# Six of sixteen states with both drive halves turned by TensorE, the other ten by GpSimd, in a Mamba scan

## The chip, the cores and the metric

The kernel runs on one core of one Trainium2 chip. The metric is the device time of one execution in microseconds. The engines are PE (TensorE, with weight loads shown as PEld), DVE (VectorE), ACT (ScalarE), POOL (GpSimd) and SP (SyncE, which here only issues DMAs). They run side by side and meet through semaphores.

## The reference

The input is x, 8 sequences of 256 tokens with 128 channels. Layer 0 is a Mamba block in both directions and a mixture of experts, layer 1 is an attention block and a second mixture. The change lies in the Mamba scan:

```python
dt = softplus(dtr @ Wdt + bdt)                  # 256 inner channels
A = -exp(Alog)                                  # 256 channels x 16 states
h = exp(dt_t * A) * h + (dt_t * u_t) * B_t      # for each of 16 states
y_t = sum over states of h * C_t
```

The first factor is called the decay here, and the product dt * u * B the drive. B and C have one value for each token and state, and dt * u one for each token and channel.

## The kernel before

**Tiling.** Tokens lie along the free axis, 512 of them (two sequences) at a time, and 128 channels on the partitions, so the 256 inner channels are two halves. Four pairs of sequences in two directions give eight groups. Each has 16 states, so `N` runs from 0 to 127 and `q = 2 N + half` counts 256 scans. State `j` is `N % 16`.

**One state.** ACT computes the decay of each half by an Exp with a scale per partition (`state`, L761). DVE scans each half over 512 tokens (`scan`, L1074): half 0 into PSUM (`ps`), half 1 into SBUF (`moe`). DVE multiplies half 0 by C (`times_c`, L1082, result `hc`) and POOL does so for half 1 (L575). PE adds both, transposed, into y (`add_y`, L1621), three states later (`LAG`). POOL counts its products in `hc_pooled`, and the scan of half 1 of state N waits until the product of state N - 2 is done, since `moe` has two buffers.

**The drives.** GpSimd makes a drive by multiplying `dtu` (dt * u) by a row of B that a DMA spread over all partitions (`drive_half`, L567). In three states of four (`turned`) half 0 comes another way: `dtuT` holds dt * u with tokens on the partitions, where B is a column, so ACT scales four blocks of 128 x 128 by a column of `bT` (`scale_drive`, L777, result `scaled`), and PE transposes them into the PSUM bank that the scan will overwrite (`turn_drive`, L1601). So a group has 12 turned halves and 20 by GpSimd.

**Order.** One list of events sets the order on every engine. PE has the events of a slot ahead of the state with that number, the other engines behind it. A slot holds the work for the next group: u at slots 0 to 3 (`part` and `u`), y of the group before at 4 and 5, z at 6 and 7 (with two table loads on ACT, L710 and L716), `finish` at 8, x at 9, dt of half 0 and 1 at 11 and 13 (DVE adds at L1057, then POOL makes `dtu`, L644), b at 14 (PE L1555, ACT L719) and t at 15 (PE L1559, ACT L721 copies into `dtuT`). In the last groups parts of the next layer's norm (`n`) and a transpose of xn (`xt`) stand in slots 10 to 14. All these share one PSUM bank, `side`. DVE multiplies the finished y by the gate (`gate_y`, L1110) inside state 3, between the two scans. A wait holds all that is behind it on its engine.

**GpSimd's order.** At state N it makes the drives of state N + 2, with the product of half 1 of state N - 1 between them.

Of the kernel before, what the change touches and what calls it, by code (L numbers as in the profile page):

```python
# [19 lines left out]
ALU = mybir.AluOpType  # L20
# [80 lines left out]
def timeline():  # L101
# [180 lines left out]
DECAYS, SB_DECAYS = 3, 2  # L282


def decay_before(q):

    n = (POOLED.index(q) - DECAYS) if pooled_drive(q) else (TURNED_Q.index(q) - SB_DECAYS)
    return -1 if n < 0 else (POOLED if pooled_drive(q) else TURNED_Q)[n]

# [5 lines left out]
def build(nc, a, out):  # L295
    with ExitStack() as ctx:
# [45 lines left out]
        dtuT = sb("dtuT", [P, COLS])  # L342
# [26 lines left out]
        drive = sb("drive", [P, DRIVES + 2, COLS])  # L369
        decay_sb = sb("decay_sb", [P, SB_DECAYS, COLS])  # L370
        scaled = sb("scaled", [P, 2, COLS])
# [71 lines left out]
        def drive_of(N, half):  # L443
            return drive[:, N % DRIVES] if half else drive[:, DRIVES + N // 4 % 2]
# [16 lines left out]
        def _(sp):  # L461
# [30 lines left out]
            def load_b(N):  # L492
                after(sp, "drive_ready", drives_before(HALVES * max(N - B_RING + 1, 0)))
                sp.dma_start(b_sb[:, N % B_RING], bc_rows[N // STATES, N % STATES].partition_broadcast(P)) \
                    .then_inc(sem[f"b_loaded{N % B_RING}"], 16)
# [20 lines left out]
            for N in range(ALL):  # L516
                if N % STATES == 0:
                    store_bc(N // STATES)
                load_b(N)
# [16 lines left out]
        def _(pool):  # L536
# [27 lines left out]
            def drive_half(N, half):  # L564
                pool.wait_ge(sem[f"b_loaded{N % B_RING}"], 16 * (N // B_RING + 1))
                after(pool, "scan_done", 2 * (N - (DRIVES if half else 8)) + half + 1)
                pool.tensor_tensor(drive_of(N, half), dtu[:, N // STATES % 2, half], b_sb[:, N % B_RING], ALU.mult) \  # L567
                    .then_inc(sem["drive_ready"], 1)
# [30 lines left out]
            for ev in MAIN_READERS:  # L599
# [18 lines left out]
                elif ev[0] == "state":  # L618
                    N = ev[1]
                    if N == 0:  # L620
                        pool.wait_ge(sem["dtu_ready"], HALVES)
                        for first in range(DRIVES - 1):
                            for half in range(HALVES):
                                if half or first and not turned(first):
                                    drive_half(first, half)
                    M = N + DRIVES - 1
                    if M < ALL:
                        if M % STATES == 0:
                            pool.wait_ge(sem["dtu_ready"], HALVES * (M // STATES + 1))
# [4 lines left out]
                    if M < ALL:  # L634
                        drive_half(M, 1)
                elif ev[0] == "dt":
# [5 lines left out]
                    if g > 1:  # L642
                        pool.wait_ge(sem["side_ready"], SIDE["t", g - 2] + 1)
# [25 lines left out]
        def _(act):  # L669
# [29 lines left out]
            def side_part(ev):  # L699
# [20 lines left out]
                elif kind == "t":  # L720
                    act.activation(dtuT[:], side, ACT.Copy).then_inc(sem["side_free"], 1)  # L721
# [45 lines left out]
            def scale_drive(N):  # L767
# [4 lines left out]
                act.wait_ge(sem["side_free"], SIDE["t", g] + 1)  # L772
# [227 lines left out]
        def _(dve):  # L1000
# [58 lines left out]
            def scan(N, half):  # L1059
                q = 2 * N + half  # L1060
                dve.wait_ge(sem["decay_ready"], q + 1)
                if half:
                    dve.wait_ge(sem["drive_ready"], drives_before(q + 1))
                    after(dve, "hc_pooled", shared_before(q) - 1)
                    source = drive_of(N, 1)
                elif turned(N):
                    dve.wait_ge(sem["drive_turned"], turned_before(N) + 1)
                    source = h_of(q)
                else:
                    dve.wait_ge(sem["drive_ready"], drives_before(q + 1))  # L1070
                    after(dve, "hc_ready", N - OWN_H + 1)
                    source = drive_of(N, 0)
# [16 lines left out]
            def state(N):  # L1089
# [7 lines left out]
                scan(N, 1)  # L1097
# [4 lines left out]
                times_c(N)  # L1102
# [366 lines left out]
        def _(pe):  # L1469
# [58 lines left out]
            def project(ev):  # L1528
# [27 lines left out]
                elif kind == "t":  # L1556
                    pe.wait_ge(sem["dtu_ready"], HALVES * g + 1)
                    for t in range(4):
                        last = pe.transpose(side[:, t * P:(t + 1) * P], dtu[:, g % 2, 0, t * P:(t + 1) * P], ident[:])  # L1559
# [32 lines left out]
            def turn_drive(N):  # L1592
# [3 lines left out]
                after(pe, "hc_ready", N - OWN_H + 1)  # L1596
                if N == 1:
                    pe.wait_ge(sem["side_free"], SIDE["dt", 0, 1] + 1)
                for t in range(4):
                    block = slice(t * P, (t + 1) * P)  # L1600
                    last = pe.transpose(ps[:, H_BANKS[N % OWN_H], block], scaled[:, n % 2, block], ident[:])  # L1601
# [420 lines left out]
```

## Time and profile before

| what | value |
|---|---|
| time, median of 3 runs | 864.05 us (862.56 to 867.24) |
| the profiled execution | 863.14 us |
| its span, from first to last instruction | 860.6 us |
| mean granted TensorE clock | 0.897 |
| PE busy | 688.3 us, 80% |
| DVE busy | 584.9 us, 68% |
| ACT busy | 601.6 us, 70% |
| POOL busy | 417.7 us, 49% |

The scan stage lies between about 120 and 578 us of the span. Busy time is the union of an engine's instructions. Starts and durations in rows of the view in order of time are microseconds from the start of the span; a bracket at a row's end tells how long its engine was idle and what ended the wait.

### The profile page before, as it was taken

To read this page: it belongs to the slowest core of one execution; us is meant where nothing else is said; L and a number is where in the kernel's file an instruction comes from. 1 tells how busy PE (TensorE), PEld (TensorE's weight loads), DVE (VectorE), ACT (ScalarE), POOL (GpSimd) and SP (SyncE) were. 2 spreads that over 40 slices of the span, in tenths; PEclk is the share of its full clock that TensorE was granted. 3 is DMA by queue.
4 is the path that set the end of the run, shared out by engine and by line. 5 is a ranking of instruction groups with operands and counts; after the bars stand their busy time and mean duration, and the time that the engine had idled before them with its cause. 6 is when DMAs were issued, how large, how long until landed. Compare 5 with 4: busy or idle time off the path is not lost.

```text
span 860.6 us, 13106 instructions
## 1 busy us (share of the span) xinstructions
PE 688.3 (80%) x4227; PEld 482.5 (56%) x4227; DVE 584.9 (68%) x851; ACT 601.6 (70%) x1235; POOL 417.7 (49%) x359
## 2 busy tenths in 40 slices
PE   5799956797886877977768675768797888888886
PEld 5588835575674565655636645767683333334433
DVE  6335669897997987979878868796325455545542
ACT  3444559878888888789887987774645667765663
POOL 4300058797896987978968778770000000000000
PEclk8889979799797997999987967889999999999998
DMA  3224525454453553644634436710200000000000
GB/s 108 99 66 132 179 100 169 135 166 144 135 186 111 156 170 119 182 137 147 189 100 142 164 109 175 249 60 1 74 26 1 1 1 1 1 1 1 13 14 24
DMA packets 48130, 85.78 MB, mean 100 GB/s; under 512 B 6320, under 2 KB 11448, under 8 KB 48064
## 3 DMA queue, kind: packets, MB, share of 16 engines
q1 hardware_dynamic: 48064, 84.96, 31.6%
q8 instruction: 34, 0.56, 0.3%
q14 instruction: 32, 0.26, 0.1%
HBM read 83.37 MB, written 1.57 MB: 99 GB/s over the span
## 4 chain that ended last, share of the span: by engine, by line
PE 34%; ACT 26%; issue 14%; DVE 10%; POOL 1%; DVEq 0%; POOLq 0%; ACTq 0%
ACT scaled L777 6%; ACT ps L761 5%; PE ps L1621 4%; ACT decay_sb L761 3%; PE ps L1570 3%; PE ps L1911 3%; PE ps L1880 2%; PE ps L1601 2%; PE ps L1888 2%; DVE ps L1074 2%; PE ps L1919 2%; PE ps L1615 2%; PE ps L1821 1%; DVE moe L1074 1%; DVE hc L1082 1%
## 5 line engine op out<-in xcount | busy, mean ns | idle before, releaser
L567 POOL TENSOR_TENSOR drive<-dtu,b_sb 128x512 f32<-128x512 f32 x160 | 203.3, 1278 | 0.7
L575 POOL TENSOR_TENSOR hc<-moe,c_sb 128x512 f32<-128x512 f32 x128 | 166.0, 1297 | 42.8 <-DVE moe L1074 42.2
L1074 DVE TENSOR_TENSOR_SCAN moe<-ps,drive 128x512 f32<-128x512 f32 x128 | 153.3, 1198 | 0.2
L1621 PEld LDWEIGHTS ps<-ident,hc 128*128 128x128 f32 x1024 | 133.2, 157 | 32.4 <-issue 27.4
L1621 PE MATMUL ps<-ident,hc 128*128 128x128 f32 x1024 | 150.7, 299 | 0.0
L1074 DVE TENSOR_TENSOR_SCAN ps<-decay_sb,ps 128x512 f32<-128x512 f32 x96 | 117.5, 1224 | 39.5 <-PE ps L1601 22.7
L981 ACT ACTIVATE probs<-ps 128x1024 f32<-128x1024 f32 (+1 forms) x96 | 87.8, 916 | 74.3 <-PE ps L1888 64.2
L1601 PE MATMUL ps<-ident,scaled 128*128 128x128 f32 x384 | 68.7, 308 | 71.3 <-ACT scaled L777 69.0
L777 ACT ACTIVATE scaled<-dtuT,bT 128x128 f32<-128x128 f32 x384 | 121.4, 389 | 0.0
L761 ACT ACTIVATE ps<-dt,negA 128x510 f32<-128x510 f32 x160 | 105.9, 676 | 1.8 <-DVE ps L1086 1.2
L580 POOL TENSOR_TENSOR stat<-stat,halfc 128x4 f32<-128x4 f32 x7 | 7.0, 1007 | 201.0 <-DVE stat L1297 201.0
L1601 PEld LDWEIGHTS ps<-ident,scaled 128*128 128x128 f32 x384 | 49.5, 157 | 85.4 <-ACT scaled L777 84.2
L1082 DVE TENSOR_TENSOR hc<-ps,c_sb 128x512 f32<-128x512 f32 x128 | 85.0, 664 | 0.0
L761 ACT ACTIVATE decay_sb<-dt,negA 128x510 f32<-128x510 f32 x96 | 68.1, 710 | 0.0
L1074 DVE TENSOR_TENSOR_SCAN ps<-ps,drive 128x512 f32<-128x512 f32 x32 | 39.2, 1225 | 22.3 <-ACT ps L761 20.0
L1911 PE MATMUL ps<-probs,v_ring 128*32 128x512 f32 x320 | 45.0, 635 | 0.0
L696 ACT ACTIVATE hT<-ps,wbuf 128x256 f32<-128x256 f32 x64 | 25.9, 472 | 22.5 <-PE ps L1672 22.5
L1880 PE MATMUL ps<-masks,ident 128*128 128x512 f16 x128 | 39.9, 394 | 0.0
L653 POOL TENSOR_TENSOR seqstat<-seqstat,halfc 128x2 f32<-128x2 f32 x8 | 5.6, 696 | 70.6 <-DVE seqstat L1221 70.6
L1919 PE MATMUL ps<-ident,avT 128*128 128x128 f32 x128 | 21.2, 290 | 18.3 <-DVE qT L1421 16.7
L1672 PE MATMUL ps<-xnT,wbuf 128*128 128x256 f32 x128 | 33.0, 406 | 0.0
L1687 PEld LDWEIGHTS ps<-wbuf,hT 128*128 128x128 f32 x256 | 30.6, 192 | 2.5 <-issue 2.0
(257 smaller groups left out, 1208.0 us busy)
## 6 DMA issues: line engine op xcount, KB each, us to landing
b_sb<-bc_rows SPq DMA_DIRECT2D x128, 256.0 KB, 3.2
c_sb<-bc_rows SPq DMA_DIRECT2D x128, 256.0 KB, 3.3
wbuf<-in_pack SPq DMA_DIRECT2D x16, 514.0 KB, 3.4
wbuf<-in_pack SPq DMA_DIRECT2D x8, 512.0 KB, 4.0
x_sb<-in_x SPq DMA_DIRECT2D x4, 256.0 KB, 3.5
out<-x_sb SPq DMA_DIRECT2D x4, 256.0 KB, 2.3
w_in<-in_w_in SPq DMA_DIRECT2D x1, 512.0 KB
bc_rows<-bcx SPq DMA_DIRECT2D x8, 64.0 KB, 2.9
```

What stands on the lines that cost most here:

```text
L567: pool.tensor_tensor(drive_of(N, half), dtu[:, N // STATES % 2, half], b_sb[:, N % B_RING], ALU.mult) \
L575: pool.tensor_tensor(hc[:, 2 * (N % DEEP) + half], h_of(q), c_sb[:, N % C_RING], ALU.mult).then_inc(sem["hc_pooled"], 1)
L761: act.activation(seqs(decay_bank(q))[:, :, lo:lo + SEQ - 1], seqs(dt[:, g % 2, half])[:, :, lo:lo + SEQ - 1], ACT.Exp, scale=negA[:, g // ...
L777: last = act.activation(scaled[:, n % 2, block], dtuT[:, block], ACT.Copy, scale=bT[:, t, j:j + 1])
L981: act.activation(probs[keys, t % 3, heads_u, 0:width], ps[keys, heads_u, 0:width], ACT.Exp, scale=HD ** -0.5).then_inc(sem["probs_ready"], 1)
L1074: dve.tensor_tensor_scan(h_of(q)[:, turn], decay_bank(q)[:, turn], source[:, turn], 0.0, ALU.mult, ALU.add).then_inc(sem["scan_done"], 1)
L1082: dve.tensor_tensor(hc[:, 2 * (N % DEEP)], h_of(q), c_sb[:, N % C_RING], ALU.mult).then_inc(sem["hc_ready"], 1)
L1601: last = pe.transpose(ps[:, H_BANKS[N % OWN_H], block], scaled[:, n % 2, block], ident[:])
L1621: last = pe.matmul(ps[:, Y_BANK + half, block], hc[:, 2 * (N % DEEP) + half, block], ident[:], start=False, stop=True, is_transpose=True, ...
L1880: pe.matmul(ps[:, kv], ident16[:], masks[:, l].unsqueeze(1).broadcast_to([P, GROUP, P]), start=True, stop=False)
L1911: last = pe.matmul(ps[g, AV_BANK + qt], v, probs[:, t % 3, kv], start=(t % 3 < 2), stop=(t % 3 != 1))
L1919: last = pe.transpose(ps[:, BACK_BANK, j * P:(j + 1) * P], avT[:, n % 2, j * P:(j + 1) * P], ident[:])
```

## The change

Six states of sixteen (`TURNED_AT`) are now turned in both halves; the other ten take both halves from GpSimd. ACT's passes are 128 x 256, one for each block of 128 tokens over both halves' channels. `dtuT` holds both halves, so the t event is split in two, one copy for each half, and the first stands ahead of b in slot 14. `dtuT` lies in `xm`. The drive of a turned state's half 1 lands in the other of the two banks for h, once DVE's product of the state before is done; PE turns it at the head of the state. In such a state DVE multiplies by C between the two scans. GpSimd makes its 20 drives of a group by a plan, up to two at each state, into one ring of six. Rows of B are loaded for the ten states alone.

```diff
-    readers += events("dt01 zero t0")
-    order += events("t0")
+    readers += events("dt01 zero t00 t01")
+    order += events("t00 t01")
...
-                          11: [("dt", n, 0)], 13: [("dt", n, 1)], 14: [("b", n)], 15: [("t", n)]})
+                          11: [("dt", n, 0)], 13: [("dt", n, 1)], 14: [("t", n, 0), ("b", n)], 15: [("t", n, 1)]})
...
+TURNED_AT = (1, 3, 6, 8, 11, 14)
+POOLED_STATES = STATES - len(TURNED_AT)
...
 def turned(N):
-    return N % 4 != 0
+    return N % STATES in TURNED_AT
...
 def turned_before(N):
-    return N - (N + 3) // 4
+    return len(TURNED_AT) * (N // STATES) + sum(j < N % STATES for j in TURNED_AT)
...
 def pooled_drive(q):
-    return q % HALVES == 1 or not turned(q // HALVES)
+    return not turned(q // HALVES)
...
-    return 2 * N - turned_before(N) + (half and not turned(N))
+    return q - HALVES * turned_before(N) - (half if turned(N) else 0)
...
+DRIVE_RING = 6
...
+def drive_plan():
+    issued, plan = 0, []
+    for e in range(ALL):
+        room = sum(POOLED[max(i - DRIVE_RING, 0)] < HALVES * e for i in range(DRIVE_RING, len(POOLED))) + DRIVE_RING
+        group, j = divmod(e, STATES)
+        known = HALVES * POOLED_STATES * (group + (2 if j >= STATES - 2 else 1))
+        needed = drives_before(HALVES * min(e + 2, ALL))
+        until = max(needed, min(issued + 2, room, known, len(POOLED)))
...
+        plan.append(POOLED[issued:until])
+        issued = until
...
-        dtuT = sb("dtuT", [P, COLS])
+        dtuT = xm[:, 4:12].rearrange("p t d -> p (t d)").rearrange("p (t c) -> p t c", c=INNER)
...
-            return decay_sb[:, turned_before(q // HALVES) % SB_DECAYS]
+            return decay_sb[:, q % HALVES]
...
+        def turned_bank(N, half):
+            return ps[:, H_BANKS[(N + half) % OWN_H]]
...
             def load_b(N):
-                after(sp, "drive_ready", drives_before(HALVES * max(N - B_RING + 1, 0)))
...
+                n = N - turned_before(N)
+                after(sp, "drive_ready", HALVES * (n - B_RING + 1))
...
             def drive_half(N, half):
...
-                after(pool, "scan_done", 2 * (N - (DRIVES if half else 8)) + half + 1)
...
+                i = drives_before(HALVES * N + half) - DRIVE_RING
+                if i >= 0:
+                    pool.wait_ge(sem["scan_done"], POOLED[i] + 1)
...
-                    M = N + DRIVES - 1
...
-                        if not turned(M):
-                            drive_half(M, 0)
-                    if N:
+                    for n, q in enumerate(DRIVE_PLAN[N]):
+                        if n == 1 and N:
+                            times_c(N - 1, 1)
+                        if q:
+                            pool.wait_ge(sem["dtu_ready"], HALVES * (q // HALVES // STATES + 1))
+                            drive_half(*divmod(q, HALVES))
+                    if N and len(DRIVE_PLAN[N]) < 2:
                         times_c(N - 1, 1)
-                    if M < ALL:
-                        drive_half(M, 1)
...
-                after(act, "drive_turned", n - 1)
+                after(act, "drive_turned", HALVES * n)
                 for t in range(4):
-                    block = slice(t * P, (t + 1) * P)
-                    last = act.activation(scaled[:, n % 2, block], dtuT[:, block], ACT.Copy, scale=bT[:, t, j:j + 1])
+                    last = act.activation(scaled[:, t], dtuT[:, t], ACT.Copy, scale=bT[:, t, j:j + 1])
...
+                if turned(N):
+                    dve.wait_ge(sem["drive_turned"], HALVES * turned_before(N) + half + 1)
+                    source = turned_bank(N, half)
...
+                if half:
+                    after(dve, "hc_pooled", shared_before(q) - 1)
+                else:
                     after(dve, "hc_ready", N - OWN_H + 1)
...
+                    if N and turned(N - 1):
+                        dve.wait_ge(sem["scan_done"], q)
...
-                scan(N, 1)
+                if turned(N):
+                    times_c(N)
+                    scan(N, 1)
+                else:
+                    scan(N, 1)
...
-            def turn_drive(N):
+            def turn_drive(N, half):
...
-                after(pe, "hc_ready", N - OWN_H + 1)
+                after(pe, "hc_ready", N - OWN_H + 1 + half)
...
                 if ev[0] == "state":
+                    if turned(ev[1]):
+                        turn_drive(ev[1], 1)
                     if ev[1] >= LAG:
                         add_y(ev[1] - LAG)
                     if ev[1] + 1 < ALL and turned(ev[1] + 1):
-                        turn_drive(ev[1] + 1)
+                        turn_drive(ev[1] + 1, 0)
```

## Rows read from the trace of the kernel before

**Rows 1.** By stretches: start:end length, busy (count) of PE, PEld, DVE, ACT, POOL, clock, DMA.

```profile
285.63:341.86 56.23, 44.23 (x262) 32.47 (x263) 48.77 (x54) 47.45 (x102) 47.33 (x39) 0.90 0.48 151
```

**Rows 2.** Waits from 172.15 to 519.41: who, for whom: us, times, longest.

```profile
PE ps L1601 <- ACT scaled L777: 46.0, 32, 4.3
...
DVE ps L1074 <- ACT ps L761: 17.9, 6, 3.0
...
DVE ps L1074 <- PE ps L1601: 17.2, 14, 3.4
```

**Rows 3.** In order of time, POOL, group 2 into 3: start, us, instruction.

```profile
283.95 1.27 POOL L644 TENSOR_TENSOR dtu<-dt,u_s 128x512 f32<-128x512 f32 x1 [1.32 <-DVE dt L1057]
285.30 1.27 POOL L567 TENSOR_TENSOR drive<-dtu,b_sb 128x512 f32<-128x512 f32 x1
286.53 1.30 POOL L575 TENSOR_TENSOR hc<-moe,c_sb 128x512 f32<-128x512 f32 x1
...
294.01 1.28 POOL L575 TENSOR_TENSOR hc<-moe,c_sb 128x512 f32<-128x512 f32 x1
```

**Rows 4.** In order of time, DVE, at ends of groups 0, 2 and 4.

```profile
169.69 0.69 DVE L1057 TENSOR_TENSOR dt<-dt_a,ps 128x512 f32<-128x512 f32 x1 [1.64 <-ACT dt_a L738]
...
183.51 1.20 DVE L1074 TENSOR_TENSOR_SCAN moe<-ps,drive 128x512 f32<-128x512 f32 x1
...
283.18 0.69 DVE L1057 TENSOR_TENSOR dt<-dt_a,ps 128x512 f32<-128x512 f32 x1 [1.20 <-ACT dt_a L738]
...
286.63 1.22 DVE L1074 TENSOR_TENSOR_SCAN ps<-decay_sb,ps 128x512 f32<-128x512 f32 x1
287.96 1.22 DVE L1074 TENSOR_TENSOR_SCAN moe<-ps,drive 128x512 f32<-128x512 f32 x1
...
395.62 0.69 DVE L1057 TENSOR_TENSOR dt<-dt_a,ps 128x512 f32<-128x512 f32 x1 [0.62 <-ACT dt_a L738]
...
408.91 1.20 DVE L1074 TENSOR_TENSOR_SCAN moe<-ps,drive 128x512 f32<-128x512 f32 x1
```

**Rows 5.** In order of time, ACT, from y's copy at slot 4 of group 3.

```profile
304.05 0.60 ACT L746 ACTIVATE moe<-ps 128x512 f32<-128x512 f32 x1 [2.29 <-issue]
304.54 0.71 ACT L761 ACTIVATE decay_sb<-dt,negA 128x510 f32<-128x510 f32 x1
...
305.76 1.26 ACT L777 ACTIVATE scaled<-dtuT,bT 128x128 f32<-128x128 f32 x4
306.94 0.58 ACT L746 ACTIVATE moe<-ps 128x512 f32<-128x512 f32 x1
...
311.58 1.28 ACT L710 ACT_TABLE_LOAD   x1
...
316.25 1.30 ACT L761 ACTIVATE ps<-dt,negA 128x510 f32<-128x510 f32 x2
```

**Rows 6.** In order of time, DVE, in the mixture of experts before the scans.

```profile
100.39 0.42 DVE L1225 TENSOR_TENSOR yg<-yg,gb 128x256 f32<-128x256 f32 x1
100.85 0.42 DVE L1226 TENSOR_TENSOR acc<-acc,yg 128x256 f32<-128x256 f32 x1
101.19 0.48 DVE L1197 SCALAR_TENSOR_TENSOR moe<-ps,cw,moe 128x256 f32<-128x256 f32 x1
```

**Rows 7.** In order of time, PE, slot 14 and state 14 of group 3.

```profile
340.15 0.60 PE L1555 MATMUL ps<-ident,bcx 16*128 16x16 f32 x4 [0.65 <-DVE dt L1057]
...
342.45 1.06 PE L1601 MATMUL ps<-ident,scaled 128*128 128x128 f32 x4
```

**Rows 8.** In order of time, PE and ACT, before the first decay of group 0.

```profile
119.21 1.12 PE L1559 MATMUL ps<-ident,dtu 128*128 128x128 f32 x4 [8.49 <-DVE dt L1057]
...
120.37 0.60 ACT L721 ACTIVATE dtuT<-ps 128x512 f32<-128x512 f32 x1 [5.85 <-PE ps L1559]
```

**Rows 9.** In order of time, DVE, state 15 of group 5.

```profile
461.17 1.23 DVE L1074 TENSOR_TENSOR_SCAN ps<-decay_sb,ps 128x512 f32<-128x512 f32 x1 [2.74 <-PE ps L1601]
```

**Rows 10.** DMA issues on the page: count, KB each, us to landing.

```profile
b_sb<-bc_rows SPq DMA_DIRECT2D x128, 256.0 KB, 3.2
```

More of the change, by code:

```diff
@@ L288, in decay_before @@
     return -1 if n < 0 else (POOLED if pooled_drive(q) else TURNED_Q)[n]
+def drive_plan():
[6 more added lines that the diff above has]
+        until = max(needed, min(issued + 2, room, known, len(POOLED)))
+        assert until <= min(known, room)
+        plan.append(POOLED[issued:until])
+        issued = until
+    assert issued == len(POOLED)
+    return plan
+DRIVE_PLAN = drive_plan()
 FIRST_USE = [[q for q in range(start, start + 12) if decay_before(q) < start] for start in (0, BACKWARD)]
@@ L368, in build @@
         e0.close()
-        drive = sb("drive", [P, DRIVES + 2, COLS])
+        drive = sb("drive", [P, DRIVE_RING, COLS])
         decay_sb = sb("decay_sb", [P, SB_DECAYS, COLS])
-        scaled = sb("scaled", [P, 2, COLS])
+        scaled = sb("scaled", [P, 4, INNER])
         h = moe[:].rearrange("p t d -> p (t d)")[:, 0:2 * COLS].rearrange("p (n c) -> p n c", n=2)
@@ L443, in drive_of @@
         def drive_of(N, half):
-            return drive[:, N % DRIVES] if half else drive[:, DRIVES + N // 4 % 2]
+            return drive[:, drives_before(HALVES * N + half) % DRIVE_RING]
+        def turned_bank(N, half):
+            return ps[:, H_BANKS[(N + half) % OWN_H]]
         def pos_bank(part):
@@ L518, in _ @@
                     store_bc(N // STATES)
-                load_b(N)
+                if not turned(N):
+                    load_b(N)
                 load_c(N)
@@ L564, in drive_half @@
             def drive_half(N, half):
-                pool.wait_ge(sem[f"b_loaded{N % B_RING}"], 16 * (N // B_RING + 1))
-                after(pool, "scan_done", 2 * (N - (DRIVES if half else 8)) + half + 1)
-                pool.tensor_tensor(drive_of(N, half), dtu[:, N // STATES % 2, half], b_sb[:, N % B_RING], ALU.mult) \
+                n = N - turned_before(N)
+                pool.wait_ge(sem[f"b_loaded{n % B_RING}"], 16 * (n // B_RING + 1))
+                i = drives_before(HALVES * N + half) - DRIVE_RING
+                if i >= 0:
+                    pool.wait_ge(sem["scan_done"], POOLED[i] + 1)
+                pool.tensor_tensor(drive_of(N, half), dtu[:, N // STATES % 2, half], b_sb[:, n % B_RING], ALU.mult) \
                     .then_inc(sem["drive_ready"], 1)
@@ L720, in side_part @@
                 elif kind == "t":
-                    act.activation(dtuT[:], side, ACT.Copy).then_inc(sem["side_free"], 1)
+                    act.activation(dtuT[:, :, half * P:half * P + P], side.rearrange("p (t c) -> p t c", c=P), ACT.Copy).then_inc(sem["side_free"], 1)
                 elif kind == "x":
@@ L1061, in scan @@
                 dve.wait_ge(sem["decay_ready"], q + 1)
[L1062 to L1068, printed above, removed]
+                if turned(N):
+                    dve.wait_ge(sem["drive_turned"], HALVES * turned_before(N) + half + 1)
+                    source = turned_bank(N, half)
                 else:
                     dve.wait_ge(sem["drive_ready"], drives_before(q + 1))
+                    source = drive_of(N, half)
+                if half:
+                    after(dve, "hc_pooled", shared_before(q) - 1)
+                else:
                     after(dve, "hc_ready", N - OWN_H + 1)
-                    source = drive_of(N, 0)
+                    if N and turned(N - 1):
+                        dve.wait_ge(sem["scan_done"], q)
                 turn = slice(None, None, -1) if N // STATES >= PAIRS else slice(None)
@@ L1101, in state @@
                         zero_boundary(q, SEQ - 1)
-                times_c(N)
+                if not turned(N):
+                    times_c(N)
             def gate_y(g):
@@ L1556, in project @@
                 elif kind == "t":
-                    pe.wait_ge(sem["dtu_ready"], HALVES * g + 1)
+                    pe.wait_ge(sem["dtu_ready"], HALVES * g + half + 1)
                     for t in range(4):
-                        last = pe.transpose(side[:, t * P:(t + 1) * P], dtu[:, g % 2, 0, t * P:(t + 1) * P], ident[:])
+                        last = pe.transpose(side[:, t * P:(t + 1) * P], dtu[:, g % 2, half, t * P:(t + 1) * P], ident[:])
                 elif kind == "z":
@@ L1590, in project_part @@
                     pe.matmul(seqs(side)[:, :, to], w_tap[:, dr, TAPS - 1 - k, cols_c], seqs(xmT[:, toks])[:, :, of], start=False, stop=False)
-            def turn_drive(N):
+            def turn_drive(N, half):
                 n = turned_before(N)
                 pe.wait_ge(sem["drive_scaled"], n + 1)
-                after(pe, "hc_ready", N - OWN_H + 1)
-                if N == 1:
+                after(pe, "hc_ready", N - OWN_H + 1 + half)
+                if n == 0 and half == 0:
                     pe.wait_ge(sem["side_free"], SIDE["dt", 0, 1] + 1)
                 for t in range(4):
-                    block = slice(t * P, (t + 1) * P)
-                    last = pe.transpose(ps[:, H_BANKS[N % OWN_H], block], scaled[:, n % 2, block], ident[:])
+                    last = pe.transpose(turned_bank(N, half)[:, t * P:(t + 1) * P], scaled[:, t, half * P:half * P + P], ident[:])
                 last.then_inc(sem["drive_turned"], 1)
```

17 lines of the change are left out of this document (4 added, 13 removed).

## The prediction

> **What bounds the kernel now.** The change touches the scan stage alone, so the first view is the one by stretches, cut at the copy of bT that ends a group of 16 states. One such group takes 56.23 us; in it DVE, ACT and POOL are busy 48.77, 47.45 and 47.33 us, PE 44.23 [rows 1]. The reader is to see four engines within 5 us of each other and all some 8 us short of the period. Nobody is full, so the order of waits decides. The view of waits says where DVE loses most over six groups: 17.9 us for ScalarE's decays in PSUM and 17.2 us for turned drives from PE [rows 2]. The wait for turned drives points at ScalarE's scaled passes (PE waited 46.0 us for them). GpSimd doesn't show in this list. But the order of time shows it: from the second dtu of a group, POOL has no gap, its eighth operation (hc of state 0) starts at 294.01 and the first at 285.30, so 1.244 us each [rows 3]. And the scan of state 15, half 1, starts at 287.96, 1.33 us behind the scan before it where 1.13 is usual; the hc before it on POOL ended at 286.53 + 1.30 = 287.83. So GpSimd already held DVE for 0.2 us there [rows 3, 4], too short a wait for the list.
>
> **What each part costs, per group.**
> ScalarE's passes. Four narrow ones take 1.17 us (305.76 to 306.94), two decays of 510 elements 1.22 us (304.54 to 305.76) [rows 5]. A pass of 128 is thus 0.29 us and one of 510 is 0.61, a slope of 0.83 ns per element; one of 256 comes to 0.40, four to 1.60 us. Bounds: 1.17 if width were free, 2.34 if a wide pass were two narrow ones. Before 12 x 1.17 = 14.1, after 6 x 1.60 = 9.6; the second copy into dtuT costs 0.49. ScalarE gets 3.9 us of its 47.5 back.
> PE: 6 x 2 turns of four replace 12 of four: nothing, but for four more transposes of dtu (0.6 us).
> GpSimd: 10 x 2 drives replace 16 + 4. The count stays 20, and with 16 hc and two dtu it keeps its 47.3 us [rows 1]. DMA loads of B rows fall from 16 to 10; the loads wait for nobody now, so nothing.
> DVE: the same 32 scans. A turned state runs scan, hc, scan, so its hc waits for the scan just ahead, and the next state's first scan waits for the turned one. What a wait on DVE's own last instruction costs: L1226 starts 0.46 us behind L1225, whose result it needs, and L1197, which needs nothing of it, 0.34 us behind [rows 6]. So 0.12 each, twice in six states, 1.4 us, where DVE is what sets the pace. The bound below is 0.
> Beside that row stands a rule of the Trainium skill (VectorE: DVE Perf Modes, The DRAIN you can't avoid): a semaphore after every operation of a chain costs nothing extra. The trace differs, 0.46 against 0.34; by the rule the 1.4 us are nil.
>
> **Where these lie on the chain.** I cut a group at its second dt add, DVE's L1057.
> (a) *dt add to the second scan of state 2 of the next group.* On DVE this took 13.82 us (169.69 to 183.51), 13.28, 14.29 and 13.29 (395.62 to 408.91) in four of the first five boundaries, and 13.82 in the fifth: mean 13.70 [rows 4]. In the new plan, worked out from the diff, GpSimd makes no drive at states 12 and 13 (nothing more may be known before the next dtu) and two at each of 14, 15, 0 and 1. The scan (2, 1) waits for hc of state 0 on GpSimd. Before, seven operations lie ahead of that hc after dtu; now ten do: drive, hc, drive three times over, and one drive. The dtu starts 0.77 behind the dt add (283.18 to 283.95), its successor 1.35 later [rows 3, 4]; 11 x 1.244 = 13.7 for the eleven; 0.13 from POOL's end to DVE's start as at 287.96. That is 15.9 us (16.0 for this one), against 13.7: **+2.2 us** at each of five boundaries, 11.0. DVE's own path there would be 0.61 + 1.25 + 0.58 + wait + 1.23 for state 14, 2.82 for 15 and for 0, 3.06 for 1 and 1.13. The wait is new too: at slot 14 PE turns dtu's half 0, ScalarE copies it, PE turns B, and only then comes the turn of state 14's second drive: some 0.1 + 0.6 + 0.6 + 0.6 + 0.9 = 2.8 us [rows 7, 8] with 1.8 us of DVE work as its cover, 0.9 left. Sum 14.4, so it is hidden by GpSimd's 15.9, and is what is late next if GpSimd is not.
> At the last two boundaries a transpose of xn stands in slot 14 as well, and DVE already waits 2.74 us there (461.17) [rows 9]; they took 15.9 and 16.1 us and stay there: 0.
> (b) *From the gate of y to the second dt add.* ScalarE waits for PE's y at slot 4 (304.05, idle 2.29) whatever lead it has, so what it saved in states 0 to 4 is lost. From there to the table load at 311.58 it scales twice before (states 6, 7: 2.34) and twice after (6, 8: 3.20): +0.86, since state 8's pass now stands ahead of the 4.67 us of table loads and silus [rows 5]. Then x, and scaled 11 +0.43, scaled 13 gone -1.17, scaled 14 +0.43; the second dt was held 0.47 by PE, which goes. Sum +0.1, with one DVE self-wait **+0.2** per group, 7 groups, 1.4. Nothing is queued for long behind the new wait of PE for half 1: hc of the state before is DVE's last act there, and two DVE instructions (1.8 us) cover a turn of 0.65.
> (c) *The start.* Slot t ran PE 119.21, ScalarE's copy 120.37, the first decay behind it [rows 8]; the second t adds a turn at 1.12 and a copy of 0.6, about 1.7 us before the first decay. State 1's second turn stands behind parts on PE, 1 us more, and ScalarE's lighter load gives some back by state 8: **+1.5**.
> (d) *Last group:* no parts; self-waits 0.7, ScalarE waits saved 0.4: +0.3.
> Sum: 11.0 + 1.4 + 1.5 + 0.3 = 14.2 us. The profiled execution took 863.14 (span 860.6 and 2.5 around it), its median is 864.05: 878.3, **878 us**.
>
> **Rivals.** Less than 0.5%, 4.3 us, can't be told from no change here.
> *1. GpSimd's cluster decides (forecast), +14, 878 us, chance 0.50.* For it: no gap on POOL in that stretch and a plan with ten operations. Against: it needs DVE to arrive within 15.9 us of the dt add.
> *2. GpSimd keeps pace, the turns at slot 14 decide.* 14.4 - 13.7 = 0.7 at five boundaries, and b, c, d: 3.5 + 3.2 = 6.7, 871 us. Chance 0.13.
> *3. The other side: ScalarE's lead.* If DVE's 17.2 us for turned drives [rows 2] are really ScalarE's load, four fifths of them may go: 864 - 14 = 850 us. For it: PE waited 46.0 us for scaled passes and 24 small passes a group fall away. Against: the waits follow table loads, x and dt, and y at slot 4 takes the lead away. It decides if hc of state 0 ends within 13.5 us of the dt add. Chance 0.13.
> The rule that speaks for it is the Trainium skill's (VectorE: DVE Perf Modes, The TRN2 errata): the fixed cost falls on each instruction, so larger tiles pay it less often. The trace agrees (0.29 for 128, 0.61 for 510 elements), which says what ScalarE saves and not whether anybody waits for it.
> *4. The two cancel*, 2 and half of 3: 6.7 - 7 = 0, 864 us, chance 0.14.
> *5. B rows come late too.* A row lands 3.2 us after issue [rows 10], and SP issues it behind the C row of the state before, which waits for an hc six states back; with drives four states ahead POOL could wait 1.3 us for it (worked out at states 3 and 5). I find it covered at the scans. If not, 1.3 at seven groups: +9, 887 us. Chance 0.10.
> Chances: slower 0.50 + 0.13 + 0.10 = 0.73, same 0.14, faster 0.13. The range leaves out rival 3 and half of 5: 862 to 886.
>
> **What would show it.** In the changed trace: six turned scans a group with source ps and result moe; the four passes into `scaled` 1.6 us together; ScalarE near 43.5 us a group; POOL without a gap from the second dtu to hc of state 0 and the scan (2, 1) of the next group 15.9 us behind the dt add (13.7 would refute a); the table load some 0.9 us later behind y's copy; the first scan 1.7 us later. I am wrong if POOL's hc of state 0 is ahead of DVE, or if the stretch from y to dt gets shorter by more than 1 us.

## The result, and the profile after

The changed kernel takes 888.03 us (885.45 to 893.62, 4 runs) and the kernel before 864.65 us (4 runs): ratio 1.0288, 95% interval 1.0257 to 1.0319. It is slower, as forecast, but by 23.4 us and not by 14. The median lies 2 us above the range.

The profiled execution took 893.62 us (span 891.8), 5.6 above the median, so stretches of its trace add up to 31.2 us against the span of 860.6. Where a stretch holds what this one execution lost more than the others, the text says so. The slower of the four are those with the lower mean granted clock (893.62 us at 0.877, 889.07 at 0.890, 886.99 at 0.891, 885.45 at 0.893).

By stretches (the group from one copy of bT to the next, the same cut as in [rows 1]; start:end length, busy and count of PE, PEld, DVE, ACT, POOL, clock, DMA share, GB/s):

```profile
291.18:350.69 59.51, 45.44 (x269) 34.33 (x270) 50.13 (x53) 43.81 (x78) 47.33 (x39) 0.87 0.38 117
```

ScalarE lost 3.6 us of work against [rows 1] (3.9 forecast), GpSimd kept its 47.33, and the group got 3.3 us longer. Relief for an engine that is not the end of the chain bought nothing.

In order of time, POOL from the second dtu to the product of state 0, for [rows 3]:

```profile
288.76 1.27 POOL L668 TENSOR_TENSOR dtu<-dt,u_s 128x512 f32<-128x512 f32 x1 [2.91 <-DVE dt L1080]
290.10 1.26 POOL L599 TENSOR_TENSOR drive<-dtu,b_sb 128x512 f32<-128x512 f32 x1
291.33 1.29 POOL L607 TENSOR_TENSOR hc<-moe,c_sb 128x512 f32<-128x512 f32 x1
292.58 2.49 POOL L599 TENSOR_TENSOR drive<-dtu,b_sb 128x512 f32<-128x512 f32 x2
...
300.01 2.50 POOL L599 TENSOR_TENSOR drive<-dtu,b_sb 128x512 f32<-128x512 f32 x2
302.47 1.28 POOL L607 TENSOR_TENSOR hc<-moe,c_sb 128x512 f32<-128x512 f32 x1
```

In order of time, DVE in the same stretch, for [rows 4]:

```profile
287.99 0.69 DVE L1080 TENSOR_TENSOR dt<-dt_a,ps 128x512 f32<-128x512 f32 x1 [0.34 <-ACT dt_a L762]
288.60 1.23 DVE L1098 TENSOR_TENSOR_SCAN ps<-decay_sb,ps 128x512 f32<-128x512 f32 x1
289.87 0.69 DVE L1106 TENSOR_TENSOR hc<-ps,c_sb 128x512 f32<-128x512 f32 x1
292.28 1.22 DVE L1098 TENSOR_TENSOR_SCAN moe<-decay_sb,ps 128x512 f32<-128x512 f32 x1 [1.72 <-PE ps L1629]
...
303.89 1.22 DVE L1098 TENSOR_TENSOR_SCAN moe<-ps,drive 128x512 f32<-128x512 f32 x1 [0.16 <-POOL hc L607]
```

Ten operations stand ahead of the product at 302.47, it ends at 303.75, and the scan (2, 1) starts at 303.89, 15.90 us behind the dt add, where step a forecast 16.0 for this boundary. But the reader is to see a second thing. The wait named for GpSimd is only 0.16 us, and 1.72 us were already lost in state 14 to PE. Two paths of nearly one length run side by side: without the 0.16 us DVE's own takes 15.7.

From the start of the scans I cut every group at the dt add, at the scan (2, 1), which is half 1 of state 2, and at the next dt add. The lengths before and after, each read from the DVE rows at its ends:

```
stretch                                   before   after   forecast of the difference
first five dt adds to scan (2, 1), sum     68.50   80.47   +11.0   measured +12.0
sixth, the same                            15.87   16.89     0     +1.0
last group, the same                       16.12   23.03     0     +6.9
six groups, (2, 1) to next dt add, sum    262.90  267.37   +1.2    +4.5
start of the scans and group 0            169.69  169.74   +1.7    0.0
last group, (2, 1) to the last scan        43.89   47.02   +0.3    +3.1
last scan to the end                      283.63  287.28     0     +3.7
```

The forecast of 1.4 for seven groups is split here into 1.2 for six and 0.2, which stands with the start's 1.5. The end is the time behind the last scan.

The last group in order of time, first SP, then POOL:

```profile
543.01 0.32 SPq L529 DMA_DIRECT2D c_sb<-bc_rows  x1
543.38 0.42 SPq L536 DMA_DIRECT2D rope<-in_rope  x1
...
549.25 1.49 SPq L538 DMA_DIRECT2D iotar<-in_iotar  x1
550.78 0.43 SPq L522 DMA_DIRECT2D b_sb<-bc_rows  x1
```

```profile
546.60 1.28 POOL L599 TENSOR_TENSOR drive<-dtu,b_sb 128x512 f32<-128x512 f32 x1
554.89 1.26 POOL L599 TENSOR_TENSOR drive<-dtu,b_sb 128x512 f32<-128x512 f32 x1 [7.01 <-issue]
```

SP issues 13 loads of the next layer's weights, 7.4 us of issuing, between a row of C and the row of B that GpSimd's drive of state 5 needs. The row is issued at 550.78 and the drive starts 4.1 us later. Behind that drive stands the product of state 0, for which DVE's scan (2, 1) waits 5.70 us:

```profile
557.50 1.22 DVE L1098 TENSOR_TENSOR_SCAN moe<-ps,drive 128x512 f32<-128x512 f32 x1 [5.70 <-POOL hc L607]
```

The label "issue" on POOL hides the DMA; the row of SP names it.

### The profile page after: what moved, and what is told of

Read it like the earlier page. It is cut to its first block and busy times, and to the rows that moved or that the text cites. A ratio compares the mean times of both kernels' runs of the same rounds, so it can differ in the third digit from the quotient of the medians.

```text
span 891.8 us, 12949 instructions
## 1 busy us (share of the span) xinstructions
PE 703.5 (79%) x4259; PEld 498.6 (56%) x4259; DVE 595.5 (67%) x851; ACT 572.5 (64%) x1051; POOL 418.0 (47%) x359
## 5 line engine op out<-in xcount | busy, mean ns | idle before, releaser
L607 POOL TENSOR_TENSOR hc<-moe,c_sb 128x512 f32<-128x512 f32 x128 | 164.9, 1291 | 10.3 <-DVE moe L1098 10.2
L1649 PEld LDWEIGHTS ps<-ident,hc 128*128 128x128 f32 x1024 | 139.3, 162 | 22.7 <-issue 19.4
L1098 DVE TENSOR_TENSOR_SCAN ps<-ps,drive 128x512 f32<-128x512 f32 x80 | 98.2, 1228 | 25.0 <-ACT ps L785 16.3
L785 ACT ACTIVATE ps<-dt,negA 128x510 f32<-128x510 f32 x160 | 103.3, 678 | 3.0 <-DVE ps L1098 1.8
L1098 DVE TENSOR_TENSOR_SCAN moe<-ps,drive 128x512 f32<-128x512 f32 x80 | 96.1, 1201 | 10.0 <-POOL hc L607 9.7
L800 ACT ACTIVATE scaled<-xm,bT 128x256 f32<-128x256 f32 x192 | 81.2, 495 | 0.0
L1098 DVE TENSOR_TENSOR_SCAN ps<-decay_sb,ps 128x512 f32<-128x512 f32 x48 | 58.8, 1225 | 28.8 <-ACT decay_sb L785 27.6
L1098 DVE TENSOR_TENSOR_SCAN moe<-decay_sb,ps 128x512 f32<-128x512 f32 x48 | 58.1, 1211 | 15.5 <-PE ps L1629 12.1
L785 ACT ACTIVATE decay_sb<-dt,negA 128x510 f32<-128x510 f32 x96 | 63.4, 709 | 0.1
L1599 PE MATMUL ps<-u_s,w_x 128*104 128x512 f32 x32 | 26.4, 974 | 19.7 <-DVE acc L1151 12.0
L1588 PE MATMUL ps<-ident,dtu 128*128 128x128 f32 x64 | 16.7, 414 | 24.7 <-DVE dt L1080 24.0
```

The lines of the kernel that those rows point to most:

```text
L607: pool.tensor_tensor(hc[:, 2 * (N % DEEP) + half], h_of(q), c_sb[:, N % C_RING], ALU.mult).then_inc(sem["hc_pooled"], 1)
L785: act.activation(seqs(decay_bank(q))[:, :, lo:lo + SEQ - 1], seqs(dt[:, g % 2, half])[:, :, lo:lo + SEQ - 1], ACT.Exp, scale=negA[:, g // ...
L800: last = act.activation(scaled[:, t], dtuT[:, t], ACT.Copy, scale=bT[:, t, j:j + 1])
L1098: dve.tensor_tensor_scan(h_of(q)[:, turn], decay_bank(q)[:, turn], source[:, turn], 0.0, ALU.mult, ALU.add).then_inc(sem["scan_done"], 1)
L1599: last = pe.matmul(ps[0:XROWS, SIDE_BANK], w_x[:, dr, h2], u_s[:, g % 2, h2], start=(h2 == 0), stop=(h2 == HALVES - 1))
L1649: last = pe.matmul(ps[:, Y_BANK + half, block], hc[:, 2 * (N % DEEP) + half, block], ident[:], start=False, stop=True, is_transpose=True, ...
```

## The experiments

Each is compared with the kernel before on its own chip. "Stretch" is dt add to the scan (2, 1) of the next group, summed over the first five in one profiled execution (80.5 us after, 68.5 before).

**e1, the plan capped; e2, rows of B two states earlier; e3, both.**

```diff
-        until = max(needed, min(issued + 2, room, known, len(POOLED)))
+        due = drives_before(HALVES * min(e + 3, ALL))
+        until = max(needed, min(issued + 2, room, known, due))
```

```diff
-                if not turned(N):
-                    load_b(N)
+                for M in ((N, N + 1, N + 2) if N % STATES == 0 else (N + 2,)):
+                    if M // STATES == N // STATES and not turned(M):
+                        load_b(M)
```

> The changed kernel with one line of the plan capped: no drive is made earlier than for state N + 2, so the burst of ten operations ahead of the product of state 0 becomes seven, as before the change. Theory A (the burst of drives at states 14, 15, 0 and 1 is the larger part of the loss): the stretch from the second dt add to the scan (2, 1) falls from 16.1 to about 14.6 us at the first five boundaries, and as rows of B are then wanted two states ahead and not four, POOL's waits for them shrink, in the last group most; 888 - 8 - 5 = 875 us. Rival B (the turn behind slot 14 or the chain from y to dt would hold the scans anyway): the stretch stays at 16 us, 885 us or more.

> The changed kernel with rows of B issued by SP two states earlier, ahead of the C rows that wait for GpSimd's products; the plan is untouched. Theory C (late rows of B behind C rows and, in the last group, behind the 13 loads of the next layer's weights are a part of their own): the stretch from dt add to scan (2, 1) falls from 23.0 to about 16 us in the last group and stays at 16 in the first five; 888 - 7 to 10 = 879 us. Theory A alone says: no change beyond 2 us, since the burst is the limit everywhere.

> Both edits, the capped plan and the rows of B two states earlier. If the burst and the late rows are two separate costs, 888 - 8 - 8 = 872 us, at least 3 us below each edit alone; if the capped plan removes the late rows too, the same as the capped plan alone within 2 us. What is left over 864 is then the chain from y to dt (4.5 us) and the turn behind slot 14 (5 x 0.9).

Measured: e1 884.96 us (ratio 1.0242, 1.0203 to 1.0281), stretch 79.5 us. e2 881.52 us (1.0206, 1.0147 to 1.0265), stretch 80.3. e3 886.67 us (1.0254, 1.0210 to 1.0298), stretch 80.3. Theory A fell: without the burst the stretch is nearly as long, and e3's forecast of 872 us missed by 15. e3 in order of time, POOL, DVE and PE:

```profile
300.94 1.28 POOL L601 TENSOR_TENSOR drive<-dtu,b_sb 128x512 f32<-128x512 f32 x1
304.19 1.29 POOL L609 TENSOR_TENSOR hc<-moe,c_sb 128x512 f32<-128x512 f32 x1 [1.97 <-DVE moe L1100]
```

```profile
288.82 0.69 DVE L1082 TENSOR_TENSOR dt<-dt_a,ps 128x512 f32<-128x512 f32 x1 [0.34 <-ACT dt_a L764]
...
293.11 1.22 DVE L1100 TENSOR_TENSOR_SCAN moe<-decay_sb,ps 128x512 f32<-128x512 f32 x1 [1.72 <-PE ps L1631]
...
300.75 1.23 DVE L1100 TENSOR_TENSOR_SCAN ps<-decay_sb,ps 128x512 f32<-128x512 f32 x1 [0.55 <-ACT decay_sb L787]
302.01 0.69 DVE L1108 TENSOR_TENSOR hc<-ps,c_sb 128x512 f32<-128x512 f32 x1
302.89 1.22 DVE L1100 TENSOR_TENSOR_SCAN moe<-decay_sb,ps 128x512 f32<-128x512 f32 x1 [0.18 <-PE ps L1631]
...
305.38 1.20 DVE L1100 TENSOR_TENSOR_SCAN moe<-ps,drive 128x512 f32<-128x512 f32 x1
```

```profile
299.18 1.04 PE L1651 MATMUL ps<-ident,hc 128*128 128x128 f32 x8
300.06 0.60 PE L1631 MATMUL ps<-ident,scaled 128*128 128x128 f32 x4
```

Now GpSimd waits for DVE, 1.97 us, and the scan (2, 1) is still 16.56 us behind the dt add: PE's turns hold it, for 1.72, 0.55 and 0.18 us. The wait of 0.55 carries ScalarE's name, but the passes of that state had ended at 299.02 and its first decay before 299.6; PE's turn of state 1's first half ended at 300.66, 0.09 ahead of the scan. It had stood behind the sums into y at 299.18. In the last group each of the three edits shortens the stretch from 23.0 to 17.2 us, as theory C said. In the medians that is 1 to 7 us (1 to 6 when each kernel is taken against the one before on its own chip), and the three don't stand apart in theirs.

**e4, state 9 turned in place of state 8, on top of e3; e13, the same on the changed kernel alone.**

```diff
-TURNED_AT = (1, 3, 6, 8, 11, 14)
+TURNED_AT = (1, 3, 6, 9, 11, 14)
```

> As with both edits, and state 9 is turned in place of state 8, so ScalarE's scaled passes for it stand behind the table loads. If their place ahead of the table loads costs (my step b, +0.86 then, 1.2 us measured in the stretch from state 5 to state 8), that stretch falls by 1.2 to 1.6 us in each of seven groups, and a part is given back at state 9, which now waits for its turn: 3 to 8 us less than both edits, 866 us. Rival: DVE waits for x behind it anyway, and the time stays within 2 us.

> The changed kernel with state 9 turned in place of state 8 and nothing else. If the scaled pass ahead of the table loads is a cost of its own, the stretch from state 5 to state 8 falls by 1.66 us in each of seven groups, as it did on top of the two other edits: 888 - 11 = 877 us. Rival: with the burst in place, GpSimd or SP takes it back behind state 8, 885 us or more.

Measured: e4 874.57 us (1.0126, 1.0088 to 1.0164), 12.1 below e3. e13 877.85 us (1.0185, 1.0144 to 1.0227), 10.2 below the changed kernel, or 8.1 when each is taken against the kernel before on its own chip. From scan (5, 0) to (8, 0) six groups take 11.12 us and not 12.78, and group 0 takes 9.58 and not 11.23: 1.66 less in each of the seven, about the length of the four scaled passes of one state (1.60 forecast from the rows, 1.70 in the row below). ScalarE in the changed kernel, in order of time, for [rows 5]:

```profile
311.51 0.60 ACT L770 ACTIVATE moe<-ps 128x512 f32<-128x512 f32 x1 [3.25 <-issue]
...
318.36 1.70 ACT L800 ACTIVATE scaled<-xm,bT 128x256 f32<-128x256 f32 x4
320.07 1.28 ACT L734 ACT_TABLE_LOAD   x1
```

The table load stands 8.56 us behind y's copy, against 7.53 in [rows 5]. No decay of state 8 can pass the 4.7 us behind it. The passes of a state placed there are paid in full.

**e5, the turn of dtu's half 0 moved to slot 15 on the changed kernel; e6, the same on top of e3.**

```diff
-                          11: [("dt", n, 0)], 13: [("dt", n, 1)], 14: [("t", n, 0), ("b", n)], 15: [("t", n, 1)]})
+                          11: [("dt", n, 0)], 13: [("dt", n, 1)], 14: [("b", n)], 15: [("t", n, 0), ("t", n, 1)]})
```

> The changed kernel with the turn of dtu's half 0 in slot 15 beside half 1 and not in slot 14; the plan of the drives, with its burst, is untouched. Theory D (two paths of equal length run side by side from the dt add to the scan (2, 1): GpSimd's burst, and the turn of state 14's second drive behind slot 14): the wait of 1.72 us in state 14 shrinks to about 0.5, and the stretch stays at 15.9 us, held by GpSimd's product of state 0; 888 us within 3. Rival (the slot alone was the limit): the stretch falls to 15 us or less, 883 us.

> The same move of the turn, with the capped plan and the early rows of B. Theory D: only now are both paths shorter, and the stretch falls from 16 to between 14.5 and 15.2 us at the first five boundaries, 5 to 7 us in all against both edits without the move. Rival (something third holds the stretch, such as ScalarE's second copy into dtuT and the scaled pass of state 1 behind it): it stays above 15.5.

Measured: e5 893.96 us (1.0354, 1.0331 to 1.0376), stretch 83.5 us. e6 877.94 us (1.0188, 1.0117 to 1.0259), stretch 75.1 us, 5.2 less than e3 and 8.7 us faster in the median (its runs spread from 871.5 to 883.3). So theory D's forecast for e6 came true in the profiled executions: with the burst capped and the turn moved the stretch is shorter, by 1.0 us each; in the medians the intervals of e3 and e6 overlap. For e5 it forecast a stretch that stays, and the sum grew. The five don't grow alike. Two are 15.93 and 15.94, as forecast, and their scans (2, 1) wait 0.98 and 0.95 us for GpSimd's product. Three are 16.98 to 17.42. They differ in TensorE's granted clock. The 15.9 us behind the dt add by stretches, for one of 17.42 and one of 15.94:

```profile
290.15:306.05 15.90, 14.47 (x65) 11.07 (x66) 12.40 (x13) 9.30 (x18) 15.05 (x13) 0.66 0.31 96
351.16:367.06 15.90, 14.47 (x79) 10.95 (x80) 14.19 (x19) 11.82 (x23) 15.06 (x13) 0.89 0.34 99
```

PE is busy for the same 14.47 us and gets 65 matmuls done at the lower clock and 79 at the higher. One of the three long ones, DVE:

```profile
237.59 1.23 DVE L1098 TENSOR_TENSOR_SCAN ps<-ps,drive 128x512 f32<-128x512 f32 x1 [1.25 <-ACT ps L785]
241.94 1.23 DVE L1098 TENSOR_TENSOR_SCAN ps<-decay_sb,ps 128x512 f32<-128x512 f32 x1 [1.43 <-ACT decay_sb L785]
```

The first wait is for a decay behind ScalarE's two copies, which waited for PE's two turns. The second again ends with PE's turn (at 241.85), and not with the decays it names (at 241.01).

The same holds in the other profiled executions. The first five stretches, with the granted clock over the 15.9 us behind their dt add (e10 and e11 follow below):

```
kernel      stretches, us (clock)
before      13.28 (1.00)  13.29 (0.99)  13.82 (0.87)  13.82 (0.80)  14.29 (0.84)
changed     15.90 (0.81)  15.92 (0.81)  15.92 (0.77)  16.15 (0.74)  16.58 (0.75)
e1          15.14 (0.89)  15.77 (0.77)  15.85 (0.79)  16.19 (0.74)  16.59 (0.79)
e3          15.64 (0.79)  15.65 (0.80)  15.84 (0.79)  16.56 (0.72)  16.58 (0.74)
e4          16.40 (0.73)  16.49 (0.72)  16.49 (0.72)  16.50 (0.72)  16.58 (0.72)
e5          15.93 (0.89)  15.94 (0.89)  16.98 (0.69)  17.18 (0.68)  17.42 (0.66)
e6          14.79 (0.87)  14.82 (0.89)  15.13 (0.85)  15.18 (0.83)  15.18 (0.83)
e7          15.18 (0.83)  15.18 (0.83)  16.60 (0.71)  16.87 (0.70)  17.22 (0.67)
e10         15.54 (0.82)  15.55 (0.82)  17.33 (0.69)  17.33 (0.69)  17.37 (0.69)
e11         13.25 (1.00)  13.26 (1.00)  14.72 (0.85)  16.11 (0.74)  16.25 (0.73)
```

So a difference of 1 or 2 us between two kernels' stretches can be the clock as much as the edit, and no run here sets the clock by itself. The change's own part can be read where the clocks are alike: 13.82 us before at 0.80 and 15.90 and 15.92 after at 0.81, the +2.2 of step a. The one stretch of e1 at 0.89 is 15.14 us where e5, with the burst, has 15.93 and 15.94 at the same clock: there the burst decides. How much of e6's gain on e3 is the edit's own stays open.

**e7, all four edits** (e6 and state 9).

> Capped plan, early rows of B, the turn moved, and state 9 turned in place of state 8. If the costs are separate, 874.6 less 5 to 7 us, 868 us; the kernel before, at 864, isn't beaten, since each turned state keeps its two waits of DVE on itself (0.35 us by the changed kernel's rows, six states, eight groups: 17 us where DVE sets the pace, say half of that).

869.20 us (1.0069, 1.0047 to 1.0090). That is 6.1 us above the kernel before on its chip (863.10), so of the 23.4 us lost about 17 are back. The forecast was 868. The stretch gave back nothing in its profiled execution: it is 81.1 us, with the clock as in the table. What e7 wins over e6 lies in the six parts from the scan (2, 1) to the next dt add, 254.8 us against 264.2.

**e8, the kernel before with DVE's order of the change in turned states:** scan, product, scan.

```diff
+                if turned(N):
+                    times_c(N)
                 scan(N, 1)
...
-                times_c(N)
+                if not turned(N):
+                    times_c(N)
```

> The kernel before with one part of the change alone: in a turned state DVE multiplies by C between its two scans, so the product waits for the scan just ahead (96 states). The row pair of before gives 0.12 us each; where DVE sets the pace (some two thirds of the states) 96 x 0.12 x 2/3 = +8 us, 872 us. Rival: nothing, within 2 us of 864, since the stalls for ScalarE and PE swallow it, or less than before, since the bank of h comes free earlier for the next turn.

870.70 us against 863.10 (1.0102, 1.0072 to 1.0133): +7.6 for 96 products that wait for the scan just ahead. DVE in order of time:

```profile
291.50 1.22 DVE L1074 TENSOR_TENSOR_SCAN ps<-decay_sb,ps 128x512 f32<-128x512 f32 x1
292.76 0.69 DVE L1082 TENSOR_TENSOR hc<-ps,c_sb 128x512 f32<-128x512 f32 x1
293.36 1.21 DVE L1074 TENSOR_TENSOR_SCAN moe<-ps,drive 128x512 f32<-128x512 f32 x1
294.50 1.20 DVE L1074 TENSOR_TENSOR_SCAN ps<-decay_sb,ps 128x512 f32<-128x512 f32 x1
```

The product starts 1.26 us behind the scan whose result it needs; the scan at 294.50 starts 1.14 behind one that it doesn't need. That is the 0.12 of [rows 6], now at 512 elements (0.14 to 0.15 against a product behind a scan that it doesn't need, which starts 1.11 to 1.12 behind in the kernel before). The rule of the Trainium skill weighed in the prediction (VectorE: DVE Perf Modes, The DRAIN you can't avoid), no cost for a semaphore between chained operations, doesn't hold for these rows; its own measurement, as the page says, is of a chain of copies. How the whole 7.6 us arises was not split further; the order also moves when banks come free.

**e9, the old order on the changed kernel; e10, the old order on e7; e11, state 13 in place of 14 on e10.**

```diff
-                if turned(N):
-                    times_c(N)
-                    scan(N, 1)
-                else:
-                    scan(N, 1)
+                scan(N, 1)
...
-                if not turned(N):
-                    times_c(N)
+                times_c(N)
```

> The changed kernel with DVE's order in a turned state put back: both scans, then the product with C. The next state's first scan then finds the scan it waits for one instruction away. By the changed kernel's rows a turned state takes 3.20 us on DVE and a pooled one 2.82, so 48 x 0.35 = 17 us if all of it were exposed, and 96 short waits of the kernel before cost 7.6 us of 11.5 possible, two thirds. Theory E (the self-waits are a third cost of the change): -8 to -11 us, 878 us. Rival: scan (N, 1) then waits for its turn on PE, whose cover shrinks from two DVE instructions to one (1.13 against 0.75 to 1.2 us at the lower clock), and nothing is gained, 886 to 890.

> The same order with the capped plan, early rows of B, the turn moved and state 9 in place of 8. Theory E: 869.2 less 8 to 11 = 860 us, and the kernel before is beaten or reached. Rival: 869 stays, since with half the states turned DVE waits for PE.

> As the kernel before this one, with state 13 turned in place of 14, so no turn of a second drive stands behind slot 14 (the turns of B and, in late groups, of xn). If what is left of the wait in state 14 (PE's turn of B, at the lower clock) costs, each of seven stretches from dt add to the scan (2, 1) falls by 0.5 to 1.2 us, more in the last two: -5 us. Rival: slot 13's dt on PE takes its place, no change.

Measured: e9 893.99 us (1.0359, 1.0309 to 1.0408), e10 872.28 us (1.0077, 1.0039 to 1.0115; 864.4 to 876.7 in 12 runs), e11 865.92 us (1.0037, 1.0010 to 1.0065; 12 runs). Theory E fell: without the self-waits the changed kernel is no faster, by its median 6 us slower. In e9 the waits for PE grow instead, in state 14 from 1.72 to 2.46 us, and the scan (1, 1) waits for its turn:

```profile
300.59 1.22 DVE L1098 TENSOR_TENSOR_SCAN ps<-decay_sb,ps 128x512 f32<-128x512 f32 x1
302.60 1.22 DVE L1098 TENSOR_TENSOR_SCAN moe<-decay_sb,ps 128x512 f32<-128x512 f32 x1 [0.79 <-PE ps L1624]
```

e11 gains 6.4 us on e10 in the median, but five of e10's twelve runs took 864.4 to 866.9 us too, at mean clocks of 0.897 to 0.907, and the other seven 871.7 to 876.7 at 0.883 to 0.894; the intervals overlap. In the profiled executions, with no second turn behind slot 14 the stretch falls to 73.6 us from 83.1, and is as low as 13.25 in two of five, those at full clock; but e10 was profiled at 873.9 us and a mean clock of 0.886, e11 at 864.1 and 0.910. It costs something ahead of the dt add: from scan (10, 0) to the dt add the first four full groups take 13.60 to 14.43 us and not 12.32 as in e10, 1.3 to 2.1 each. It is the best version with this way of making the drives and does not beat the kernel before.

**e12, the 13 weight loads behind the last row of C.**

```diff
-                if N == ALL - STATES + 4:
+                if N == ALL - 1:
                     load_l1()
```

> The changed kernel with the 13 loads of the next layer's weights issued behind the last row of C and not in state 4 of the last group; everything else as in the changed kernel. Theory C (in the last group GpSimd's drive of state 5 waited 7.0 us because SP issued 13 loads ahead of its row of B): the stretch from dt add to the scan (2, 1) of the last group falls from 23.0 to 16 to 17 us and the kernel from 888 to 881 to 882. Rival: the row of B is late by itself behind the row of C, the stretch stays above 20 us.

884.33 us (1.0261, 1.0216 to 1.0306), 3.7 below the changed kernel by the medians, or 1.6 when each is taken against the kernel before on its own chip; the intervals overlap. In the profile the last group's stretch is 17.24 us and not 23.03, and from there to the last scan it takes 45.5 us and not 47.0. The 13 loads were the cause of those 5.8 us of the stretch. The gate of y follows the last scan after 4.9 us and not 8.5, but that is not the loads: in e13, where they stand as in the changed kernel, it is 4.8, and in e3, whose last stretch is 17.23, it is 9.3. In the 5 us behind the last scan the granted clock is 0.50 in the changed kernel and in e3, 0.66 in e13 and 1.00 in e12. By stretches, the changed kernel and then e13:

```profile
604.52:609.52 5.00, 5.00 (x25) 5.00 (x26) 3.00 (x8) 0.28 (x1) 1.37 (x2) 0.50 0.00 0
591.65:596.65 5.00, 5.00 (x32) 5.00 (x32) 3.70 (x11) 0.28 (x1) 1.39 (x2) 0.66 0.01 3
```

A later drive still waits 3.36 us for its row of B, now with the right name:

```profile
557.59 1.28 POOL L599 TENSOR_TENSOR drive<-dtu,b_sb 128x512 f32<-128x512 f32 x1 [3.36 <-DMA b_sb<-bc_rows]
```

## Why the prediction was wrong in size

**Step a, right in its sum, wrong in what stands behind it.** 15.9 us at each boundary were forecast and 15.90 to 16.58 measured. "DVE's own path" was put at 14.4 and is 15.7. The term that failed is the wait in state 14: 0.9 us forecast, 1.72 measured. I took the turn of dtu at 0.6 us, though [rows 8] has the same work at 1.12, and that of state 14 at 0.9; each took 1.11. In this stretch the granted clock is 0.50, 1.2 of 2.4 GHz, as it is from 284 on. PE was busy for 1.59 of the 4 us from 284 to 288, and its wait for the dt add, at 288.73, was 2.1 us long. By stretches of the changed kernel, and three turns in order of time:

```profile
288.00:291.00 3.00, 1.58 (x8) 1.18 (x8) 2.52 (x3) 1.78 (x3) 2.17 (x2) 0.50 0.23 67
291.00:293.00 2.00, 2.00 (x11) 1.96 (x11) 0.72 (x1) 1.41 (x3) 2.00 (x3) 0.50 0.00 0
298.00:302.00 4.00, 4.00 (x22) 2.77 (x23) 3.97 (x5) 2.77 (x5) 4.00 (x4) 1.00 0.42 143
```

```profile
288.73 1.11 PE L1588 MATMUL ps<-ident,dtu 128*128 128x128 f32 x4 [2.08 <-DVE dt L1080]
291.07 1.11 PE L1629 MATMUL ps<-ident,scaled 128*128 128x128 f32 x4
...
300.14 0.60 PE L1629 MATMUL ps<-ident,scaled 128*128 128x128 f32 x4
```

Most of the rest of the 1.3 us is DVE's waits on itself, 0.12 us more than forecast behind state 14 and 0.14 in state 1. With the burst capped, PE's turn of state 1's first half can be late as well, by 0.55 in one of e3's five stretches, where the clock stood at 0.50 for 9 us behind the dt add. So the path that the prediction named as late next was nearly as long as GpSimd's, and undoing the burst alone gave 0.9 us in five stretches at most. The base of 13.7 was itself a mean over two clocks: 13.3 at full clock, 13.8 to 14.3 below it.

**Step b, too small by 3 us.** +0.2 per group was forecast, +0.74 measured, as a sum of terms of both signs. Its first term, +0.86 for the pass ahead of the table loads, measured +1.2 in its stretch, and e13 shows that this place of the passes alone is worth 8 to 10 us over the kernel. I credited its removal elsewhere (state 13) against it without asking what the kernel would do with neither. In e13 the six parts take 256.1 us, 6.8 less than before the change, where the changed kernel takes 4.5 more.

**Step c** was 1.5 and is 0.0: the first scan is 2.5 us later, and group 0 makes it good. First scans of one profiled execution each vary from 120.6 to 124.2 us between edits that don't touch the start, so a single one does not show it.

**Step d failed, and is the largest single part of the error.** +0.3 was forecast for the last group and nothing for its boundary; 3.1 and 6.9 us were measured, 9.7 of the 17.0 us by which the profiled execution missed the forecast. It is rival 5's mechanism, a row of B that comes late, at the place where I did not look: I priced it at a wait of 1.3 us, from the 3.2 us of a landing, and overlooked what SP's queue holds between a row of C and the next row of B in the last group. The plan asks for drives up to four states ahead, and SP's order was not moved with it. In the kernel before, SP ran the same 13 loads and GpSimd waited for no row of B in this group. e12 took back 5.8 us of the boundary and 1.6 behind it in the profile, but only 1.6 to 3.7 us in the median, of the 10 by which the median missed.

The 3.7 us behind the last scan, for which nothing was forecast, are not the change's but this execution's. The gate of y comes 3.3 us later there than before, at a clock of 0.50 against 0.68. In e13, whose last group has the same late row (a stretch of 22.95 us), the time behind the last scan is 284.0 us, 0.3 more than before.

**The rivals.** Rival 3 (a gain from ScalarE's relief) is refuted by the group's 43.81 us of ScalarE work in 59.51. Rival 2 by itself is what e1 shows, but at 80 us for the five stretches and not at 72. Self-waits of DVE cost 0.12 for the product and 0.2 for the scan behind a scan (1.34 against 1.13), where 0.12 each was forecast. The kernel before gets slower with 96 of the first kind (e8). What they cost in the changed kernel e9 can't tell, since waits for PE take their place.

What stays open: what sets the clock in a stretch, and how much of the change's loss comes by a lower clock. Whether a better set of turned states beats the kernel before was tried for two places only.

## What to carry to other kernels

When one wait is removed from a stretch, compute the next path through it with the same care, durations at the clock of that very stretch included: with paths of 15.9 and 15.7 us side by side, neither e1 nor e5 alone shortened the stretches by more than 1 us in all. Before two stretches are compared, their clocks are: the same code took 15.2 us at 0.83 and 17.2 at 0.67 (e7). A wait that carries one engine's name can end with another's work; the row that ends just ahead of it decides. Work taken from an engine pays only where the engine's queue is the chain; what counts is what stands ahead of its longest block, here four scaled passes of 1.6 us together ahead of the table loads. Who makes a producer run further ahead has to move its loads in the DMA queue too, and walk that queue to the end of the program.

## What was not expected of the hardware

A tensor_tensor of DVE on 512 elements that needs the result of the instruction just ahead starts 1.26 us behind it, where a scan that doesn't need it starts 1.14 behind; a scan that waits for the scan just ahead starts 1.34 us behind it, where 1.13 is usual. TensorE stood at half clock over the 9 us from 284 to 293 of the changed kernel, busy for 5.2 of them, and four transposes took 1.11 us there and 0.60 at full clock.
